# Experts and router logits of an attention and mixture-of-experts block: fp32 words multiplied whole in place of three products of halves

## What is computed

```python
x = x + xattn(layernorm(x), ctx, ...)          # 16 batches of 100 rows, 256 wide, 16 heads, causal
h = layernorm(x).reshape(-1, 256)              # 1600 rows
scores = sigmoid(h @ gate_w.T)                 # 32 experts; biased, grouped by 4, best 4 of 8 groups, best 8 experts
combine = ...                                  # weight of each expert for each row, 0 where it was not chosen
g = silu(einsum('th,eih->tei', h, w_gate))     # w_gate, w_up: 32 x 128 x 256
u = einsum('th,eih->tei', h, w_up)
routed = einsum('tei,ehi->th', g * u * combine[:, :, None], w_down)
shared = (silu(h @ sh_gate.T) * (h @ sh_up.T)) @ sh_down.T      # as two more experts of 128
x = x + routed + shared
```

## Time and profile before

| | us |
|---|---|
| runs of the kernel before (3) | 728.13, 731.82, 741.09; median 731.82 |
| profiled execution, first to last instruction (span) | 725.5 |
| expert stage in it, first `gate_up` in the loop to the last `down` matmul | 240.4 to 721.6 |
| TensorE busy | 663.4 (91%) |
| VectorE busy | 583.5 (80%) |

### The profile page before, as it was taken

How to read it: one execution, slowest core, us unless ns; L and a number is a source line. 1 busy time by engine, 2 the same in 40 slices (tenths; PEclk the granted TensorE clock), 3 DMA queues, 4 the chain that set the end, 5 groups by cost and what they waited for, 6 DMA issues and landing times.

```text
span 725.5 us, 13617 instructions
## 1 busy us (share of the span) xinstructions
PE 663.4 (91%) x3952; PEld 618.7 (85%) x3952; DVE 583.5 (80%) x1053; ACT 316.2 (44%) x831; POOL 229.1 (32%) x203
## 2 busy tenths in 40 slices
PE   2989999999983999999999999999999999999996
PEld 2988888888863899999999999989999999999996
DVE  4886888888738688888888888888888888888886
ACT  3437777777611333334333333433343333334332
POOL 5321122222200333333333433333333333333332
PEclk9999999999966799999999999999999999999999
DMA  5222222222101344343434334353424333342431
GB/s 177 82 60 58 59 53 59 50 59 62 52 1 46 81 124 110 112 118 103 132 97 125 104 118 115 106 154 114 123 98 133 97 125 105 116 121 100 132 97 67
DMA packets 53813, 69.72 MB, mean 96 GB/s; under 512 B 22856, under 2 KB 35216, under 8 KB 53796
## 3 DMA queue, kind: packets, MB, share of 16 engines
q1 hardware_dynamic: 53796, 69.51, 33.3%
HBM read 61.08 MB, written 1.86 MB: 87 GB/s over the span
## 4 chain that ended last, share of the span: by engine, by line
PE 70%; DVE 11%; issue 8%; ACT 7%; DMA 2%; POOL 1%; DVEq 0%; SPq 0%; ACTq 0%; POOLq 0%
PE ps L805 43%; PE ps L990 23%; DVE nm L601 4%; ACT prob L437 4%; ACT pt_hi L442 2%; PE ps L867 1%; DVE h L629 1%; DMA x_g<-x 1%; DVE pt_lo L611 1%; PE ps L852 1%; DVE nm_scaled L605 1%; DMA cst<-consts 1%; DVE h_lo_all L652 1%; DVE xn L556 1%; ACT h_hi_all L452 0%
## 5 line engine op out<-in xcount | busy, mean ns | idle before, releaser
L384 POOL TENSOR_TENSOR act<-act,cw 128x400 f32<-128x400 f32 x136 | 178.9, 1315 | 320.0 <-DVE act L750 314.9
L503 ACT ACTIVATE act<-ps 128x400 f32<-128x400 f32 x136 | 68.7, 505 | 304.8 <-PE ps L805 304.8
L805 PE MATMUL ps<-h_hi_all,w_hi 128*128 128x400 f32 x544 | 189.0, 347 | 5.2 <-DVE w_lo L699 5.2
L805 PE MATMUL ps<-h_lo_all,w_hi 128*128 128x400 f32 x544 | 188.8, 347 | 0.0
L805 PE MATMUL ps<-h_hi_all,w_lo 128*128 128x400 f32 x544 | 188.6, 347 | 0.0
L747 DVE SCALAR_TENSOR_TENSOR act<-act,ps 128x400 f32<-128x400 f32 x136 | 77.7, 571 | 78.6 <-ACT act L503 78.6
L990 PE MATMUL ps<-a_hi,w_hi 128*128 128x400 f32 x272 | 98.7, 363 | 19.4 <-issue 17.0
L805 PEld LDWEIGHTS ps<-h_hi_all,w_hi 128*128 128x128 f32 x544 | 103.1, 190 | 5.8 <-issue 5.8
L805 PEld LDWEIGHTS ps<-h_lo_all,w_hi 128*128 128x128 f32 x544 | 103.1, 190 | 0.0
L805 PEld LDWEIGHTS ps<-h_hi_all,w_lo 128*128 128x128 f32 x544 | 103.1, 190 | 0.0
L699 DVE TENSOR_TENSOR w_lo<-w_raw,w_hi 128x512 fp32r<-128x512 f32 x68 | 102.8, 1512 | 0.0
(11 more groups left out here) (134 smaller groups left out, 914.3 us busy)
## 6 DMA issues: line engine op xcount, KB each, us to landing
cw<-combine_rows SPq DMA_DIRECT2D x68, 400.0 KB, 4.1
w_raw<-w_exp SPq DMA_DIRECT2D x68, 256.0 KB, 3.9
w_raw<-w_exp SPq DMA_DIRECT2D x68, 128.0 KB, 2.0
k_blocks<-k_all SPq DMA_DIRECT2D x128, 25.0 KB, 2.0
q_now<-q_all SPq DMA_DIRECT2D x16, 200.0 KB, 2.8
x_g<-x SPq DMA_DIRECT2D x4, 400.0 KB
ctx_f<-ctx_t SPq DMA_DIRECT2D x4, 400.0 KB, 4.5
x_r<-x SPq DMA_DIRECT2D x16, 100.0 KB
```

Source lines behind the costliest of these rows:

```text
L384: pool.tensor_tensor(act[:, s, :], act[:, s, :], cw[:, (s // 2) % 2, (s % 2) * TG:(s % 2 + 1) * TG], ALU.mult).then_inc(weighted, 1)
L503: a.activation(act[:, s, :], ps[:, 4 + 2 * (s % 2), 0:TG], ACT.Tanh, scale=0.5).then_inc(tanh_e, 1)
L805: last = t.matmul(out, w, m, start=(i == 0), stop=(i == n - 1))
```

## The change

The cut into halves goes away for the expert weights, the normalised rows, the activations and the router weights. TensorE is given the fp32 words as they stand in SBUF, and each product is one matmul instruction of fp32 operands instead of three of fp32r. So `gate_up` issues 4 matmuls in place of 12, `down` 2 in place of 6, and each call of `logits` 2 in place of 6. The tensors `h_hi_all` and `h_lo_all` become `h_all`; `w_hi`, `w_lo`, `a_hi`, `a_lo`, `wg_hi`, `wg_lo` and their semaphores go. The waits move to what is left: TensorE waits for the landing of the weights and for `weighted`, the SP queue for `gu_psum` and `down_done` before it loads a slot again, ScalarE for `down_done` of four steps before. Projections and attention keep their halves, apart from the last copy of each batch (`norm_low`). The core of the diff:

```diff
 
         x1t_all = keep("x1t_all", [P, KC, T])
-        h_hi_all = keep("h_hi_all", [P, KC, T], F32R)
-        h_lo_all = keep("h_lo_all", [P, KC, T], F32R)
...
-        w_hi = keep("w_hi", [P, 2, 3 * D], F32R)
-        w_lo = keep("w_lo", [P, 2, 3 * D], F32R)
         cw = keep("cw", [P, 2, CPH * TG])
         act = keep("act", [P, 4, TG])
-        a_hi = keep("a_hi", [P, 4, TG], F32R)
-        a_lo = keep("a_lo", [P, 4, TG], F32R)
...
-                    wait_alone(sp, gu_lo, E - 1, half_ready, 1)
+                    wait_alone(sp, gu_psum, CPH * (E - 1), half_ready, 1)
                     gate_up_load(e + slot, slot)
-                    wait_alone(sp, dn_lo, E - 1, half_ready, 1)
+                    wait_alone(sp, down_done, CPH * (E - 1), half_ready, 1)
                     down_load(e + slot, slot)
                     wait_alone(sp, weighted, CPH * (E - 1), half_ready, 1)
                     combine_loads(h, e + slot, slot)
...
-            a.wait_ge(gate_in, 16)
-            a.activation(wg_hi[:], wg[:], ACT.Copy).then_inc(w_hi_ready, 1)
...
                 a.wait_ge(ht_psum, B + 1)
-                a.activation(h_hi_all[:, :, batch_cols(B)], ps[:, 5, 0:KC * S].rearrange("p (k q) -> p k q", k=KC),
-                             ACT.Copy).then_inc(h_hi_ready, 1)
+                a.activation(h_all[:, :, batch_cols(B)], ps[:, 5, 0:KC * S].rearrange("p (k q) -> p k q", k=KC),
...
-            def split_gu(loaded, slot):
-
-                a.wait_ge(wr_in[slot], 16 * loaded)
-                a.activation(w_hi[:, slot, 0:2 * D], w_raw[:, slot, 0:2 * D], ACT.Copy).then_inc(gu_hi, 1)
-
-            def split_dn(loaded, slot):
-                a.wait_ge(wd_in[slot], 16 * loaded)
-                a.activation(w_hi[:, slot, 2 * D:], w_raw[:, slot, 2 * D:], ACT.Copy).then_inc(dn_hi, 1)
-
             def lead(N, s, pair):
                 a.wait_ge(gu_psum, N + 1)
                 a.activation(act[:, s, :], ps[:, 4 + 2 * (s % 2), 0:TG], ACT.Tanh, scale=0.5).then_inc(tanh_e, 1)
 
-            def split(N, s, pair):
-
-                if s % 2 == 1:
-                    split_dn(pair + 1, s // 2)
-                elif not (isinstance(N, int) and N // 2 + 1 >= HALVES * NX):
-                    split_gu(pair + 1 + s // 2, (s // 2 + 1) % 2)
-
-            def lag(N, s):
-                a.wait_ge(weighted, N + 1)
-                a.activation(a_hi[:, s, :], act[:, s, :], ACT.Copy).then_inc(a_hi_ready, 1)
+            def a_turn(N, s):
+                if not (isinstance(N, int) and N < 4):
+                    a.wait_ge(down_done, N - 3)
+                lead(N, s, 0)
 
             a.wait_ge(half_out, 16)
-            split_gu(1, 0)
             lead(0, 0, 0)
-            split(0, 0, 0)
...
-            with a.Fori(0, total // 4 - 1) as p:
+            for k in range(4):
+                a_turn(k + 1, (k + 1) % 4)
+            with a.Fori(1, total // 4 - 1) as p:
                 for s in range(4):
                     k = 4 * p + s
-                    lead(k + 1, (s + 1) % 4, p + (s + 1) // 4)
-                    lag(k, s)
-                    split(k + 1, (s + 1) % 4, p + (s + 1) // 4)
-            for k in range(total - 4, total):
-                if k + 1 < total:
-                    lead(k + 1, (k + 1) % 4, (k + 1) // 4)
-                lag(k, k % 4)
-                if k + 1 < total:
-                    split(k + 1, (k + 1) % 4, (k + 1) // 4)
+                    a_turn(k + 1, (s + 1) % 4)
+            for k in range(total - 4, total - 1):
+                a_turn(k + 1, (k + 1) % 4)
 
 
...
-            v.wait_ge(w_hi_ready, 5)
-            v.tensor_tensor(wg_lo[:], wg[:], f(wg_hi[:]), ALU.subtract).then_inc(w_lo_ready, 1)
...
-            def norm_low(B):
-                v.wait_ge(x1t_ready, B + 1)
-                v.tensor_tensor(h_lo_all[:, :, batch_cols(B)], ps[:, 5, 0:KC * S].rearrange("p (k q) -> p k q", k=KC),
-                                f(h_hi_all[:, :, batch_cols(B)]), ALU.subtract).then_inc(h_lo_ready, 1)
...
-            def split_gu(count, slot):
-                v.wait_ge(gu_hi, count)
-                v.tensor_tensor(w_lo[:, slot, 0:2 * D], w_raw[:, slot, 0:2 * D], f(w_hi[:, slot, 0:2 * D]),
-                                ALU.subtract).then_inc(gu_lo, 1)
...
-                split_gu(1, 0)
...
-            def split_at(pair, s, last=False):
-                if s % 2 == 1:
-                    slot = s // 2
-                    v.wait_ge(dn_hi, 2 * pair + slot + 1)
-                    v.tensor_tensor(w_lo[:, slot, 2 * D:], w_raw[:, slot, 2 * D:], f(w_hi[:, slot, 2 * D:]),
-                                    ALU.subtract).then_inc(dn_lo, 1)
-                elif not last:
-                    split_gu(2 * pair + s // 2 + 2, (s // 2 + 1) % 2)
-
-            def lag(N, s):
-                v.wait_ge(a_hi_ready, N + 1)
-                v.tensor_tensor(a_lo[:, s, :], act[:, s, :], f(a_hi[:, s, :]), ALU.subtract).then_inc(a_lo_ready, 1)
...
-                    t.wait_ge(h_lo_ready, B)
+                    t.wait_ge(x1t_ready, B)
...
-            t.wait_ge(w_lo_ready, 5)
+            t.wait_ge(w_lo_ready, 4)
+            t.wait_ge(gate_in, 16)
...
             def logits(c):
-                t.wait_ge(h_lo_ready, BG * (c + 1) + 1)
+                t.wait_ge(x1t_ready, BG * (c + 1) + 1)
                 cols = slice(c * TG, (c + 1) * TG)
-                product(ps[0:NE, c, 0:TG], [(wg_hi[:, k, :], wg_lo[:, k, :], h_hi_all[:, k, cols], h_lo_all[:, k, cols])
-                                            for k in range(KC)]).then_inc(lt_psum, 1)
+                for k in range(KC):
+                    last = t.matmul(ps[0:NE, c, 0:TG], wg[:, k, :], h_all[:, k, cols], start=k == 0, stop=k == KC - 1)
+                last.then_inc(lt_psum, 1)
...
-            def gate_up(N, s, col, experts):
+            def gate_up(N, s, col, loaded):
                 slot = s // 2
                 if s % 2 == 0:
-                    t.wait_ge(gu_hi, experts)
-                    t.wait_ge(gu_lo, experts)
+                    t.wait_ge(wr_in[slot], 16 * loaded)
                 if not (isinstance(N, int) and N < 2):
                     t.wait_ge(gated, N - 1)
                 for part_of in range(2):
-                    w = lambda a, k: a[:, slot, (2 * part_of + k) * P:(2 * part_of + k + 1) * P]
-                    last = product(ps[:, 4 + 2 * (s % 2) + part_of, 0:TG],
-                                   [(w(w_hi, k), w(w_lo, k), h_hi_all[:, k, col:col + TG], h_lo_all[:, k, col:col + TG])
-                                    for k in range(KC)])
+                    for k in range(KC):
+                        at = (2 * part_of + k) * P
+                        last = t.matmul(ps[:, 4 + 2 * (s % 2) + part_of, 0:TG], w_raw[:, slot, at:at + P], h_all[:, k, col:col + TG],
+                                        start=k == 0, stop=k == KC - 1)
                 last.then_inc(gu_psum, 1)
 
-            def down(k, s, experts):
+            def down(k, s, loaded):
                 slot = s // 2
                 if s % 2 == 0:
-                    t.wait_ge(dn_hi, experts)
-                    t.wait_ge(dn_lo, experts)
-                t.wait_ge(a_hi_ready, k + 1)
-                t.wait_ge(a_lo_ready, k + 1)
+                    t.wait_ge(wd_in[slot], 16 * loaded)
+                t.wait_ge(weighted, k + 1)
                 for m in range(KC):
-                    w = lambda a: a[:, slot, 2 * D + m * P:2 * D + (m + 1) * P]
-                    for i, (ww, mm) in enumerate(((w_hi, a_hi), (w_hi, a_lo), (w_lo, a_hi))):
-                        last = t.matmul(ps[:, (s % 2) * KC + m, 0:TG], w(ww), mm[:, s, :], start=False, stop=False,
-                                        skip_group_check=True)
+                    last = t.matmul(ps[:, (s % 2) * KC + m, 0:TG], w_raw[:, slot, 2 * D + m * P:2 * D + (m + 1) * P], act[:, s, :],
+                                    start=False, stop=False, skip_group_check=True)
                 last.then_inc(down_done, 1)
 
             t.wait_ge(tanh_ready, 1)
@@ -1013,13 +943,13 @@
 
                 with t.Fori(h * STEPS // 4, (h + 1) * STEPS // 4 - 1) as p:
                     for s in range(4):
-                        gate_up(4 * p + s + 2, (s + 2) % 4, col(s % 2, 0), 2 * p + s // 2 + 2)
-                        down(4 * p + s, s, 2 * p + s // 2 + 1)
+                        gate_up(4 * p + s + 2, (s + 2) % 4, col(s % 2, 0), p + s // 2 + 1)
+                        down(4 * p + s, s, p + 1)
                 for s in range(4):
                     N = (h + 1) * STEPS - 4 + s
                     if N + 2 < total:
-                        gate_up(N + 2, (s + 2) % 4, col(s % 2, 1 if s >= 2 else 0), N // 2 + 2)
-                    down(N, s, N // 2 + 1)
+                        gate_up(N + 2, (s + 2) % 4, col(s % 2, 1 if s >= 2 else 0), (N + 2) // 4 + 1)
+                    down(N, s, N // 4 + 1)
 
 
 # ---- launch: one core; inputs and outputs as the reference has them ----
```

(25 more changed lines are left out.)

2 lines of the change are left out of this document (removed).

## The result

The changed kernel took 799.29 us (median of 4 runs, 788.34 to 801.09) against 732.2 for the kernel before in the same runs. The ratio is 1.0859, with a 95% interval of 1.0764 to 1.0953: 8.6% slower. Two later sets on other occasions gave 1.0916 (1.0877 to 1.0955) and 1.0894 (1.0841 to 1.0947).

What follows compares the result with a forecast made beforehand. The prediction took TensorE's pace in the expert stage, plus one stall a pair, as the bound. Span 725.5 + 67.0 - 6.5 - 0.6 + 0.4 = 785.8 us, plus 6.3 to the median, gave 792 us, range 780 to 842.

Steps and rivals of the forecast that it cites:

- The product of whole words: Expert matmuls: a product of whole fp32 words takes four streams, 0.674 us, against 0.546 for three fp32r matmuls.
- upper end: Expert matmuls: highest price of a whole-word product, four fp32r matmuls at the pace seen, 0.727 us.
- The pair and the stage: Expert stage: a pair of steps takes 8.09 us, the stage 548.2 against 481.2, growing by 67.0 us.
- The gap before `down`: Expert stage: TensorE's wait for the low half of the down weights, 0.5 us a pair, goes.
- Transfers: Expert weight loads: issued later but hidden with 3 us over, 97 GB/s needed; cost zero.
- Attention: End of each attention batch: `norm_low` leaves and TensorE's waits for it go, 6.5 us less, bounds 0 and 8.
- Routing and logits: Routing chain loses a cut of gate weights, minus 0.6 us; logits become 8 whole-word matmuls, plus 0.4 us.
- The step from the span to the median: Whole kernel: the median of the runs lies 6.3 us over the span of the profiled execution.
- Two cycles a column: Rival, expert products: 0.337 us each, loads 0.9 us late, 4.9 us a pair, 577 us in all; chance 8%.
- Exposed weight loads: Rival, expert products: weight loads show once or twice a product, 0.11 us each, 880 to 970 us; chance 6%.
- The granted clock in the stage: Rival, expert stage: a lower granted clock makes products take 1.33 us; a fifth of the stage gives 900 us; chance 3%.
- No change: Rival, whole kernel: products cost 0.60 us or less, the vanished gap and `norm_low` pay for it, 730 us; chance 3%.

Runs made afterwards that it cites:

- ordinary matmuls by the identity: The kernel before with the 256 transposes of the probabilities issued as matmuls by the identity; 735.37 us in one run.
- four-halves kernel: The kernel before with the fourth product of halves (lo by lo) added in the experts; 844.47 us in one run.
- third profile: The changed kernel run again without any change, for the third time; median 794.27 us, profiled span 787.8 us.
- one stream: The kernel before with only the product of the high halves kept in the experts; span 521.4 us.
- bf16 kernel: The kernel before with the low half of the down weights cut on GpSimd and low-half products as bf16 matmuls; 701.05 us, ratio 0.9626 to the kernel before.

## Why the prediction was right, point by point

- **The product of whole words.** Forecast 2 x (0.333 + 0.0035) = 0.674 us, measured 0.672. The rule of four passes that I cited from the Trainium skill ("FP8 and Floating Point Precision", section TensorE Precision Notes) now has its rows: two listed matmuls of 0.336, each two cycles a column. That I doubled the transposes' price was right in part by luck: I put their half price down to the identity's entries, and it belongs to the kind of instruction, as the kernel with ordinary matmuls by the identity shows. The four-halves kernel shows the upper end, 0.726, to be another thing.
- **The pair and the stage.** 8.09 us forecast, 8.06 measured; 548.2 us of stage forecast, 545.6 measured. The break-even of 0.590 us a product was not reached.
- **The gap before `down`.** It went, and nothing came late in its place; TensorE is busy 180.00 of 180. I had its cause half right: VectorE's L756 was late, but for two thirds of its 1.28 us it waited for GpSimd. At the end of the kernel TensorE idles 0.3 us where I had 0.9.
- **Transfers.** Cost zero, as forecast. GpSimd waits for `cw` in the changed kernel, as the view of waits shows (us in total, times, longest), but TensorE is never idle for it in the stretch above:

```profile
POOL act L376 <- DMA cw<-combine_rows: 228.2, 64, 4.2
```

- **Attention.** Forecast 6.5 us less. From the first scores of the loop to the first logits it is 155.2 us before, 148.7 in the third profile of the changed kernel and 153.6 with `norm_low` back: 4.9 us belong to `norm_low`. The kernel before had 3.4 us at the lower clock there; where 20.5 us of it made attention 9.5 us longer, 3.4 would make 1.6, which is the rest (an estimate). So the 6.5 us came out, but as the wait for `norm_low` they were about a third too large. I had missed what comes next: the sign that I gave, `turn` waiting for `x1t_all`, did not come, and TensorE now waits for VectorE's low half of the transposed probabilities, for which the kernel before sat idle 1.6 us in all. In the first profile of the changed kernel (us in total, times, longest):

```profile
PE ps L814 <- DVE pt_lo L578: 5.9, 14, 1.0
```

- **Routing and logits.** The chain from tanh to the first transposes of the combine weights is 15.8 us in place of 16.4, the 0.6 forecast. Logits cost 1.3 to 2.0 us more, where I had 0.4. That term was mis-sized in the working: by its own prices 24 x 0.182 = 4.4 us become 8 x 0.674 = 5.4, which is 1.0 more. Besides, they run partly at 1.2 GHz, and there a product takes 1.33 us (from 212.48 to 213.81 us in the first profile).
- **The sum.** 785.8 us of span forecast; 787.8 measured where the clock held in attention, 792.9 and 798.5 where it did not for 17.1 and 20.5 us. Added up for the first profile: 3.9 us in the projections before attention begins (54.3 against 50.3; the kernels here begin it at 50.3 to 54.4 whatever they change), 9.5 in attention (158.2 us, against 148.7 in the third profile, which has no lower clock there, and in my sum) and 1.6 in logits, less 2.6 in the stage, is 12.4 of 12.7 us. The step from the span to the median, 6.3 us, was wrong in kind: where the record has the span of a run of the kernel before, the run lies 1.8 us above it, and of the changed kernel 2.2 us; the rest of the 6.3 was how executions differ. By luck it stood for the lower clock, which the sum did not have: 792 forecast, medians of 794.3 to 799.3 measured.
- **Rivals.** Two cycles a column did not come, though what I held against it, that an identity needs one part alone, was wrong. Its time, 577 us, may have been priced too high: with one stream a pair took 4.0 us, near TensorE's own 4.04 for two, and not 4.9. By that my estimate would be some 525 us, but no run shows it, for in that kernel a slot of weights is free when ScalarE has cut it, and in the changed one only when TensorE has multiplied it, which is what the 0.9 us stood for. Exposed weight loads did not come: each load is 0.19 us and lies under 0.336. The granted clock in the stage is 1.00. No change did not come.

## What to carry to other kernels

Before you replace split products by whole words, count streams: here three fp32r matmuls cost 0.546 us, one product of whole words 0.672, and no relief of other engines can pay for that once TensorE is busy throughout. Look then for what makes TensorE wait; here it was one 0.4 us cut that stood behind another engine's 1 us, and moving it was worth 4.5%, about half of what the change cost. When an instruction takes three times what its size asks, see what ran beside it before you call it slow.

## What the runs showed of the hardware

- A product of fp32 words is listed as two matmuls. Each takes two cycles a column at 2.4 GHz plus 2 to 5 ns (0.336 us for 400 columns, 0.088 for 100). A transpose of fp32 words is one such (0.086 to 0.087 us for 100 columns).
- A matmul of 400 columns with 128 new weights took 0.180 to 0.184 us, fp32r or bf16, though its columns need 0.167. Whole words show nearly none of this excess. What it is stays open; the bf16 kernel excludes the width of the words and the listed time of the weight load.
- VectorE's fp32 operations with two SBUF inputs and GpSimd's multiplication of SBUF tensors take turns, instruction by instruction: 0.44 us became 1.28, and in the other order 0.57 became 1.41.
- The same program ran attention's first batches at 1.2 GHz for 20.5, 17.1 and 0 us in three executions. The 20.5 us made attention 9.5 us longer, the 17.1 us 7.9 (158.2 and 156.6 us against 148.7).
